# One weight for the present token and a constant for the past sums, in the read-out of a recurrence

## The reference, cut to what matters

```python
def step(carry, kv_t):
    p, q, o = carry
    no = jnp.maximum(o, u + kt)
    A = jnp.exp(o - no)
    E = jnp.exp(u + kt - no)
    y = (A * p + E * vt) / (A * q + E)
    no2 = jnp.maximum(w + o, kt)
    A2 = jnp.exp(w + o - no2)
    E2 = jnp.exp(kt - no2)
    return ((A2 * p + E2 * vt, A2 * q + E2, no2), y)
```

## Time and profile before

| | |
|---|---|
| time, median of 3 runs | 810.92 us (809.68 to 814.71) |
| span of the profiled execution | 806.8 us; its own device time isn't given |
| middle turns | six, about 89 us each |
| TensorE | busy 741.4 us (92%) |
| VectorE | busy 633.1 us (78%), 1043 instructions |
| ScalarE | busy 384.9 us (48%), 730 instructions |
| POOL | busy 398.0 us (49%), 382 instructions |
| mean granted TensorE clock | 0.975 |

### The profile page before, as it was taken

How to read it: one execution, slowest core, us unless ns; L and a number is a source line. 1 busy time by engine, 2 the same in 40 slices (tenths; PEclk the granted TensorE clock), 3 DMA queues, 4 the chain that set the end, 5 groups by cost and what they waited for, 6 DMA issues and landing times.

```text
span 806.8 us, 13118 instructions
## 1 busy us (share of the span) xinstructions
PE 741.4 (92%) x4582; PEld 642.7 (80%) x4582; DVE 633.1 (78%) x1043; ACT 384.9 (48%) x730; POOL 398.0 (49%) x382
## 2 busy tenths in 40 slices
PE   6988799889999999989998999989998999968896
PEld 5876687778888788878887888878887988746785
DVE  2857589687978798888989798888979797899532
ACT  3536434556355644654455645653465635431321
POOL 1024332364746365464636465455546464565364
PEclk8999979999999999999999999999999999988999
DMA  8170002010022013110032113110121000101121
GB/s 249 53 208 1 1 1 53 27 54 27 27 79 67 27 38 81 45 47 13 26 78 66 35 30 78 55 37 26 43 74 53 26 26 26 41 26 40 34 73 51
DMA packets 35895, 41.19 MB, mean 51 GB/s; under 512 B 3118, under 2 KB 27096, under 8 KB 35864
## 3 DMA queue, kind: packets, MB, share of 16 engines
q1 hardware_dynamic: 35864, 40.78, 17.6%
HBM read 36.45 MB, written 4.33 MB: 51 GB/s over the span
## 4 chain that ended last, share of the span: by engine, by line
PE 59%; DVE 15%; issue 4%; POOL 3%; ACT 1%; DMA 1%; DVEq 0%; POOLq 0%; ACTq 0%
PE sums L475 14%; PE gate_ps L475 13%; PE up_ps L475 12%; PE transit L475 6%; DVE wk L1389 3%; DVE wk L1394 3%; PE transit L540 3%; PE transit L467 3%; PE transit L552 3%; DVE wk L1396 2%; POOL act_sb L1139 2%; PE transit L520 1%; POOL hid_l L1130 1%; DVE act_sb L1379 1%; DVE za_l L1333 1%
## 5 line engine op out<-in xcount | busy, mean ns | idle before, releaser
L1130 POOL TENSOR_TENSOR hid_l<-act_sb,hid_h 128x512 fp32r<-128x512 f32 (+1 forms) x128 | 173.3, 1354 | 171.9 <-ACT hid_h L917 171.9
L917 ACT ACTIVATE hid_h<-act_sb 128x512 fp32r<-128x512 f32 (+1 forms) x128 | 80.4, 628 | 150.9 <-POOL act_sb L1139 117.8
L1139 POOL TENSOR_TENSOR act_sb<-act_sb,late 128x512 f32<-128x512 f32 x64 | 92.0, 1438 | 100.2 <-DVE act_sb L1381 80.9
L1379 DVE SCALAR_TENSOR_TENSOR act_sb<-act_sb,gate_ps 128x512 f32<-128x512 f32 (+1 forms) x128 | 85.8, 670 | 68.9 <-ACT act_sb L901 68.9
L475 PE MATMUL sums<-down_h,hid_h 128*128 128x256 f32 x320 | 92.3, 288 | 12.7 <-POOL hid_l L1130 12.7
L475 PE MATMUL sums<-down_h,hid_l 128*128 128x256 f32 x320 | 90.0, 281 | 0.0
L475 PE MATMUL sums<-down_l,hid_h 128*128 128x256 f32 x320 | 90.0, 281 | 0.0
L1381 DVE TENSOR_TENSOR act_sb<-act_sb,up_ps 128x512 f32<-128x512 f32 x120 | 82.4, 687 | 4.1
L901 ACT ACTIVATE act_sb<-gate_ps 128x512 f32<-128x512 f32 x80 | 47.2, 590 | 71.4 <-PE up_ps L475 66.1
L475 PEld LDWEIGHTS sums<-down_h,hid_h 128*128 128x128 f32 x320 | 60.9, 190 | 19.8 <-issue 17.9
L475 PE MATMUL gate_ps<-zm_h,gate_h 128*128 128x512 f32 x140 | 62.3, 445 | 5.6 <-DVE act_sb L1381 5.6
(11 more groups left out here) (194 smaller groups left out, 1962.7 us busy)
## 6 DMA issues: line engine op xcount, KB each, us to landing
late<-combine_rows SPq DMA_DIRECT2D x64, 256.0 KB, 3.2
ctx_tok<-in_ctx SPq DMA_DIRECT2D x8, 512.0 KB, 4.9
vals<-in_ctx SPq DMA_DIRECT2D x16, 256.0 KB, 5.6
out_x<-late SPq DMA_DIRECT2D x8, 512.0 KB, 3.2
xa<-in_x SPq DMA_DIRECT2D x7, 512.0 KB, 3.5
wk<-in_L_ffn_w SPq DMA_DIRECT2D x2, 682.0 KB
late<-in_L_ffn_w_down SPq DMA_DIRECT2D x1, 1024.0 KB, 6.6
wk<-in_L_ffn_w_gate SPq DMA_DIRECT2D x2, 512.0 KB, 4.4
```

Source lines behind the costliest of these rows:

```text
L917: nc.scalar.activation(hid_h[0:n, pos], act_sb[0:n, pos], ACT.Copy).then_inc(hid_h_set, 1)
L1130: nc.gpsimd.tensor_tensor(hid_l[0:n, pos], act_sb[0:n, pos], hid_h[0:n, pos].bitcast(F32), ALU.subtract).then_inc(hid_l_set, 1)
L1139: nc.gpsimd.tensor_tensor(act_sb[:, pos], act_sb[:, pos], comb_sb[:, pos], ALU.mult).then_inc(weighted, 1)
L1379: nc.vector.scalar_tensor_tensor(mine, mine, 1.0, gate_ps[pos][0:hidden_rows(chunk)], ALU.add, ALU.mult).then_inc(gated_one, 1)
```

## The change

The reference's y does not change if numerator and denominator are both divided by the same number. The changed kernel reads out y = (c p + R v) / (c q + R), with R = exp(k - OMAX of the token before + min(u, 0)) and c = exp(-max(u, 0)), which is one number per channel. So DELTA, its two clamps and one of the two exponentials go. R's argument is a subtraction that POOL makes in `inputs`; the part of u goes in as the bias of the exponential, as the decay now does for A2. The products with c and the sums are one instruction each. The pad of k ahead of each sequence becomes -17 instead of -1e38, so that R stays finite at the first token, and min(u, 0) is kept above -70. In turn 0 VectorE splits u in two instructions on 128x2, and ScalarE makes c with one.

In the diff below the declarations of semaphores are left out, as are the same replacements in the other turns; `read_states` and `add_now` become `add_states` where `add_now` stood, in each of them, and the calls of `clamps` go.

```diff
-        OMAX, A2, E2, EV, DELTA, EA, EE = range(7)
+        OMAX, A2, E2, EV, NUM, RV, R = range(7)
...
             def decays(t, h):
                 act.wait_ge(a2arg_set, t.count("W", KH, h + 1))
-                nc.scalar.activation(seqs(h, A2, 1), seqs(h, A2, 1), ACT.Exp).then_inc(a2_set, 1)
+                nc.scalar.activation(seqs(h, A2, 1), seqs(h, A2, 1), ACT.Exp, bias=decay_sb[:, h:h + 1]).then_inc(a2_set, 1)
...
             def readouts(t, h):
-                act.wait_ge(clamp_set, t.count("W", 2 * KH, 2 * h + 2))
-                nc.scalar.activation(flat(h, EA)[:, 0:TOK], flat(h, EA)[:, 0:TOK], ACT.Exp, scale=-1.0).then_inc(ea_set, 1)
-                nc.scalar.activation(flat(h, EE)[:, 0:TOK], flat(h, EE)[:, 0:TOK], ACT.Exp).then_inc(ee_set, 1)
+                act.wait_ge(rarg_set, t.count("W", KH, h + 1))
+                nc.scalar.activation(flat(h, R)[:, 0:TOK], flat(h, R)[:, 0:TOK], ACT.Exp, bias=bonus_now[:, h:h + 1]).then_inc(r_set, 1)
+
+            def bonus_weight():
+                act.wait_ge(bonus_split, 1)
+                nc.scalar.activation(bonus_past[:], bonus_past[:], ACT.Exp, scale=-1.0).then_inc(bonus_set, 1)
...
                 nc.gpsimd.tensor_tensor(seqs(h, E2, 1), kw[:, h, :, 1:S1], seqs(h, OMAX, 1), ALU.subtract).then_inc(e2arg_set, 1)
+                nc.gpsimd.tensor_tensor(in_seqs(flat(h, R)), kw[:, h, :, 1:S1], seqs(h, OMAX, 0), ALU.subtract).then_inc(rarg_set, 1)
...
             def weigh_now(t, h):
-                pool.wait_ge(ee_set, t.count("W", KH, h + 1))
-                pool.wait_ge(scans_done, t.count("W", 2 * KH, 2 * h + 2))
-                nc.gpsimd.tensor_tensor(seqs(h, A2, 1), flat(h, EE)[:, 0:TOK].rearrange("p (b s) -> p b s", b=NS),
-                                        vw[:, h].rearrange("p (b s) -> p b s", b=NS), ALU.mult).then_inc(eev_set, 1)
+                pool.wait_ge(r_set, t.count("W", KH, h + 1))
+                nc.gpsimd.tensor_tensor(flat(h, RV)[:, 0:TOK], flat(h, R)[:, 0:TOK], vw[:, h], ALU.mult).then_inc(rv_set, 1)
...
-                nc.vector.memset(kw[:, :, :, 0:1], NEG)
+                nc.vector.memset(kw[:, :, :, 0:1], K_LEAST)
+                nc.vector.tensor_scalar(bonus_now[:], bonus_sb[:], 0.0, U_LEAST, ALU.min, ALU.max)
+                nc.vector.tensor_scalar(bonus_past[:], bonus_sb[:], 0.0, None, ALU.max).then_inc(bonus_split, 1)
...
             def exponents(t, h):
                 dve.wait_ge(omax_set, t.count("W", KH, h + 1))
-                nc.vector.scalar_tensor_tensor(seqs(h, A2, 1), seqs(h, OMAX, 0), decay_sb[:, h:h + 1], seqs(h, OMAX, 1),
-                                               ALU.add, ALU.subtract).then_inc(a2arg_set, 1)
-                nc.vector.scalar_tensor_tensor(flat(h, DELTA)[:, 0:TOK].rearrange("p (b s) -> p b s", b=NS), kw[:, h, :, 1:S1],
-                                               bonus_sb[:, h:h + 1], seqs(h, OMAX, 0), ALU.add, ALU.subtract).then_inc(delta_set, 1)
-
-            def clamps(t, h):
-
-                dve.wait_ge(delta_set, t.count("W", KH, h + 1))
-                nc.vector.tensor_scalar(flat(h, EA)[:, 0:TOK], flat(h, DELTA)[:, 0:TOK], 0.0, None, ALU.max).then_inc(clamp_set, 1)
-                nc.vector.tensor_scalar(flat(h, EE)[:, 0:TOK], flat(h, DELTA)[:, 0:TOK], 0.0, None, ALU.min).then_inc(clamp_set, 1)
+                nc.vector.tensor_tensor(seqs(h, A2, 1), seqs(h, OMAX, 0), seqs(h, OMAX, 1), ALU.subtract).then_inc(a2arg_set, 1)
...
-            def read_states(t, h):
-
-                dve.wait_ge(ea_set, t.count("W", KH, h + 1))
+            def add_states(t, h):
+
+                past = bonus_past[:, h:h + 1]
+                dve.wait_ge(rv_set, t.count("W", KH, h + 1))
                 dve.wait_ge(scans_done, t.count("W", 2 * KH, 2 * h + 2))
-                nc.vector.tensor_tensor(in_seqs(flat(h, DELTA)), in_seqs(flat(h, EA)), seqs(h, EV, 0), ALU.mult).then_inc(ap_set, 1)
-                nc.vector.tensor_tensor(in_seqs(flat(h, EA)), in_seqs(flat(h, EA)), seqs(h, E2, 0), ALU.mult).then_inc(aq_set, 1)
-
-            def add_now(t, h):
-
-                dve.wait_ge(eev_set, t.count("W", KH, h + 1))
-                dve.wait_ge(ap_set, t.count("W", KH, h + 1))
-                nc.vector.tensor_tensor(in_seqs(flat(h, DELTA)), in_seqs(flat(h, DELTA)), seqs(h, A2, 1), ALU.add).then_inc(num_set, 1)
-                dve.wait_ge(aq_set, t.count("W", KH, h + 1))
-                nc.vector.tensor_tensor(flat(h, EE)[:, 0:TOK], flat(h, EA)[:, 0:TOK], flat(h, EE)[:, 0:TOK], ALU.add).then_inc(den_set, 1)
+                if t.fixed and t.i == LAG["W"] and h == 0:
+                    dve.wait_ge(bonus_set, 1)
+                nc.vector.scalar_tensor_tensor(in_seqs(flat(h, NUM)), seqs(h, EV, 0), past, in_seqs(flat(h, RV)), ALU.mult, ALU.add).then_inc(num_set, 1)
+                nc.vector.scalar_tensor_tensor(in_seqs(flat(h, R)), seqs(h, E2, 0), past, in_seqs(flat(h, R)), ALU.mult, ALU.add).then_inc(den_set, 1)
...
                 m_gate(3)
-                for h in range(KH):
-                    clamps(t, h)
                 m_gate(4)
                 for h in range(KH):
                     scans(t, h)
-                for h in range(KH):
-                    read_states(t, h)
                 m_gate(5)
-                add_now(t, 0)
+                add_states(t, 0)
                 divide(t, 0, 0)
                 divide(t, 0, 1)
                 m_gate(6)
                 quotient(t, 0)
-                add_now(t, 1)
+                add_states(t, 1)
```

More of the change, by code:

```diff
@@ L27 @@
 NEG = -1e38
+K_LEAST = -17.0
+U_LEAST = -70.0
 TRANSIT = [
@@ L151, in build @@
         bonus_sb = sb("bonus_sb", [P, KH])
+        bonus_now = sb("bonus_now", [P, KH])
+        bonus_past = sb("bonus_past", [P, KH])
         abs_sum = sb("abs_sum", [P, 3])
@@ L204, in seqs, with in_seqs @@
             return flat(h, c).rearrange("p (b s) -> p b s", b=NS)[:, :, first:first + S]
-        OMAX, A2, E2, EV, DELTA, EA, EE = range(7)
+        def in_seqs(part):
+            return part[:, 0:TOK].rearrange("p (b s) -> p b s", b=NS)
+        OMAX, A2, E2, EV, NUM, RV, R = range(7)
         late = sb("late", [P, 3 * NT * D])
@@ L220, in build @@
         rank = sb("rank", [P, NT])
-        beats, ties = (flat(1, c)[:, 0:NT * E * E].rearrange("p (r e f) -> p r e f", r=NT, e=E) for c in (DELTA, EA))
+        beats, ties = (flat(1, c)[:, 0:NT * E * E].rearrange("p (r e f) -> p r e f", r=NT, e=E) for c in (NUM, RV))
         ranks = sb("ranks", [P, NT, E])
@@ L254, in build @@
             sem("za_h_set"), sem("zm_h_set"), sem("smax_set"), sem("nsmax_set"), sem("rinv_set"), sem("rgain_set"), sem("vw_set"))
[L255 to L260, removed]
+        omax_set, a2arg_set, e2arg_set, rarg_set = (
+            sem("omax_set"), sem("a2arg_set"), sem("e2arg_set"), sem("rarg_set"))
+        a2_set, e2_set, r_set, ev_set, scans_done, rv_set = (
+            sem("a2_set"), sem("e2_set"), sem("r_set"), sem("ev_set"), sem("scans_done"), sem("rv_set"))
+        num_set, den_set, dinv_set, yw_set = (
+            sem("num_set"), sem("den_set"), sem("dinv_set"), sem("yw_set"))
+        bonus_split, bonus_set = sem("bonus_split"), sem("bonus_set")
         lmax_set, pexp_set, route_chain, combine_set, combT_out = (
@@ L989, in turn @@
                     act.wait_ge(tern_set, 3)
+                    bonus_weight()
                 f_chunk(0)
@@ L1410, in scans @@
                 nc.vector.tensor_tensor_scan(flat(h, E2), flat(h, A2), flat(h, E2), 0.0, ALU.mult, ALU.add).then_inc(scans_done, 1)
[L1412 to L1417 removed]
+            def add_states(t, h):
+                past = bonus_past[:, h:h + 1]
+                dve.wait_ge(rv_set, t.count("W", KH, h + 1))
                 dve.wait_ge(scans_done, t.count("W", 2 * KH, 2 * h + 2))
[L1419 to L1428 removed]
+                if t.fixed and t.i == LAG["W"] and h == 0:
+                    dve.wait_ge(bonus_set, 1)
+                nc.vector.scalar_tensor_tensor(in_seqs(flat(h, NUM)), seqs(h, EV, 0), past, in_seqs(flat(h, RV)), ALU.mult, ALU.add).then_inc(num_set, 1)
+                nc.vector.scalar_tensor_tensor(in_seqs(flat(h, R)), seqs(h, E2, 0), past, in_seqs(flat(h, R)), ALU.mult, ALU.add).then_inc(den_set, 1)
             def divide(t, h, piece):
[L1432 removed]
+                part = flat(h, R)[:, piece * TOK // 2:(piece + 1) * TOK // 2]
                 dve.wait_ge(den_set, t.count("W", KH, h + 1))
@@ L1438, in quotient @@
                 dve.wait_ge(num_set, t.count("W", KH, h + 1))
-                nc.vector.tensor_tensor(vw[:, h], flat(h, DELTA)[:, 0:TOK], flat(h, EE)[:, 0:TOK], ALU.mult).then_inc(yw_set, 1)
+                nc.vector.tensor_tensor(vw[:, h], flat(h, NUM)[:, 0:TOK], flat(h, R)[:, 0:TOK], ALU.mult).then_inc(yw_set, 1)
             def add_recurrence(t):
@@ L1509, in turn @@
                     decay_rows()
-                if w:
-                    for h in range(KH):
-                        clamps(t, h)
                 m_gate(4)
@@ L1523, in turn @@
```

(6 more changed lines are left out.)

3 lines of the change are left out of this document (removed).

## The result

The changed kernel takes 817.59 us (median of 20 runs, 807.67 to 821.59 but for one of 1439.49), the kernel before beside it 811.82 us (808.52 to 814.71). The ratio is 1.0052, 95% interval 1.0029 to 1.0074: half a per cent slower, within the 1% that the forecast called no change. It leaves out five slow runs of the changed kernel, four of 820.22 to 821.59 us and the one of 1439.49. The median lies 3.4 us above the 814.2 forecast. The profiled execution took 817.39 us, of which 815.7 are its span; the span before was 806.8. So 8.9 us of span are to be explained; the medians are 5.8 us apart.

A forecast was written before the change was run, and what follows sets the result against it. The prediction took TensorE as the bound in middle turns (92% busy over the span) and VectorE in the closing turn. Terms +2.5 + 7.5 - 2.0 - 4.7 = +3.3 made span 810.1, plus 4.1 around it 814.2 us; range 803.5 to 819.5.

The forecast's parts named there:

- POOL's wait: Middle turns, ahead of `down(2)`: TensorE's two waits become one of 3.1 us on POOL, +2.5 us in six turns.
- POOL's slot: POOL's queue ahead of `low_hidden(2)` in middle turns: two added subtractions end it 2 x 1.20 us later.
- The count of what meets what: Middle turns: POOL's instructions taking turns with VectorE's stay three, so each added subtraction takes 1.2 us, not 2.0.
- The clock: Middle turns, behind the 3.1 us wait: half rate in about five of six, 1.5 us each, +7.5 us.
- Turn 1: Turn 1, between the last scan and `add_attention`: four instructions become two, -2.0 us, with ends 1.2 and 3.9.
- The closing turn: Closing turn, ahead of gates 5 and 7: both `read_states` go and scans end earlier, -4.7 us, ends 3 and 7.
- kept to the end: Closing turn: the 4.7 us gain lasts, because the rest hangs on gate 7 behind the same VectorE queue.
- Around the span: Time outside the profiled span: the median's 810.92 - 806.8 = 4.1 us, added to the forecast span of 810.1.
- At nothing: Middle turns: removing `clamps`, `read_states` and `add_now` beside full TensorE rows is worth nothing; the bias exponential priced as now.
- The clock holds: Rival, middle turns: the longer wait comes but TensorE stays at 2.4 GHz; -4.2 us, 806.7 us, chance 0.20.
- POOL collides: Rival, ahead of `low_hidden(2)`: added subtractions cost 2.0 us each, wait 4.6 us; +19, 830 us, chance 0.10.
- Nothing reaches the end: Rival, all turns: TensorE sets them, POOL's delay fits its wait, VectorE's gains meet other waits; 810.9 us, chance 0.08.

The follow-up runs named there:

- the traced-again run with the wait on VectorE: Kernel before with only POOL's `low_hidden` of chunk 2 moved ahead of its two `inputs` subtractions, traced a second time: 817.32 us, once.
- the filled wait: Changed kernel with 11 small products with zeros run by TensorE in the middle turns' wait ahead of the down product of chunk 2: 803.27 us, ratio 0.9906.
- the right order: Changed kernel with `low_hidden(2)` ahead of `inputs` on POOL and the added subtractions on VectorE behind gate 4, in the middle turns: 788.32 us, ratio 0.9728.

## Why the prediction was right

- **POOL's wait: right.** One wait of 3.11 us ahead of `down(2)` (forecast 3.1), on POOL, none ahead of the query products. POOL's slot grew by 2.49 us (8.11 - 5.62), against 2.40, and it began where it did, 3.14 us behind the copy of the keys against 3.12. The count of what meets what was right too: three of POOL's instructions met one of VectorE's, as before (2.24, 1.75 and 1.75 us), and the two more met none, at 1.27 us each instead of the 1.2 assumed. The last of these is `low_hidden(2)`, which took 1.72 us before. Moving the subtractions out, and adding them alone, both bear out the slot. The cost at full clock was 1.7 us in six turns, against 2.5.
- **The clock: right in kind, too small in size.** This is the term that was mis-sized: +7.5 us became +12.6. Six falls came, not five. The step that failed is the length of the slow stretch: the forecast took 3.4 us of half rate for every fall, though its rows also held one of 5.9. Three of the six lasted 3.4 us and cost 1.2 to 1.5 us, as priced; the other three lasted 6.8 and cost 2.8 each. In the traced-again run with the wait on VectorE, all three falls were of 3.4 us and cost 1.6 (mean 90.42 against 88.83).
- **Turn 1: right, but its size is not settled.** `add_attention` begins 20.59 us behind the copy of the keys, where it began at 22.48, -1.9 us against the forecast 2.0. At the next copy 2.2 us were left; but with the same code there, turn 1 took 67.4 to 70.2 us in other executions, and the old turn 1 took 70.8 to 73.2. Slow stretches behind TensorE's idle times in it differ between executions. The stretch ahead of it took 90.7 to 95.2 us in the twelve traces, so its -1.4 is no gain of the change.
- **The closing turn: the mechanism right, the end of it missed.** Gate 7 came 5.05 us earlier (37.54 us behind the copy instead of 42.59), against 4.7. That it would be "kept to the end" failed: behind gate 9 TensorE waited 1.98 us for the last norm and 0.66 for POOL, the clock was 0.50 from 756 to 764, and the logits' products and the last sums ran at half rate. The forecast had the clock in its sum for the middle turns alone. In the eight traces with VectorE's relief the end took 103.3 to 107.5 us, in the four without it 108.9 to 113.0.
- **Around the span:** 4.1 us was assumed, 1.7 measured (817.39 - 815.7), and 1.7 to 1.9 in every other run. The forecast set a median beside the span of one short execution: with 1.7 us around it, that one took an estimated 808.5 us, the low end of the kernel's 808.52 to 814.71. The span was forecast 5.6 us too short (815.7 - 810.1), and this gave 2.4 of them back. That the time still lies in the range is in part this chance; six of the 20 runs lie above its 819.5.
- **At nothing, and it was:** the removal of `clamps`, `read_states` and `add_now` beside full TensorE rows. The exponential with a bias was priced as one without and wasn't: 716 ns against 622 in the means over 16 each. A row of that kind stood in the trace before: the tanh (L901), 682 ns with a scale per partition and 590 without. The Trainium skill (ScalarE: Activation LUTs, What ACT_TABLE_LOAD costs) has about 93 ns more for an operand that is a pointer to one value per partition, and the traces agree with 94 and 92. ScalarE was not the bound, and no cost of it shows.
- **The rivals.** "The clock holds" is what the filled wait shows: 803.27 us against its 806.7. "POOL collides" needed VectorE's old instructions in the slot. With them the wait grew to 4.05 us against its 4.6, and a turn by 3.4 against its 4.3; that 829.12 comes near its 830 is chance, since the 830 holds 6.7 us of gains in other turns that this version doesn't have. "Nothing reaches the end" fell: VectorE's relief is worth 23 us with the right order (811.62 - 788.32), 13.5 of them in the middle turns, and the order without it nothing, although TensorE is busiest by far. The Trainium skill (Perfetto Trace Analysis, Identifying the Most-Contended Engine) says to optimize the engine with the highest occupancy first, and to judge TensorE by how much of its peak it reaches and by its weight loads instead of its matmuls. Its weight loads are 80% busy against VectorE's 78%, so TensorE comes first that way too. Read as the prediction read it, with 0 for VectorE's relief, the rule fails in these traces: a turn that is full elsewhere still waits for VectorE at one place.

## What to carry to other kernels

When work moves from one engine to another, look at what stands behind its new place in that engine's queue: two subtractions of 1.3 to 1.8 us ahead of one that TensorE waited for cost more than VectorE's shorter queue gave. When a wait goes, follow the queue of the engine that was late to the next thing it makes, and look whether the moved work is now ahead of that. And price a wait of TensorE together with the clock behind it: here 0.3 us of delay a turn came with 2.1 us of slow clock in the mean, and idle products in the wait took the second away without touching the first.

## What the hardware did that was not expected

Two waits of TensorE of about 3 us (3.11 and 3.06) differ in what follows: half rate in 18 of 18 turns for the one, in 3 of 12 for the other, and what decides isn't shown. Half rate also came behind a wait of 1.91 us in one middle turn of six, with the subtractions on VectorE. It lasted 3.4 us in three middle turns of the changed kernel and 6.8 in the other three, behind waits of nearly the same length (2.95 to 2.98 us and 2.87 to 3.11). And a subtraction on POOL takes 1.27 us alone and 1.71 to 1.77 beside VectorE instructions with two inputs in SBUF, which themselves go from 0.68 to 1.7: the two engines finish such work one after the other.
